# Counting edges into a table: the running counts re-added by TensorE, copied back by ScalarE, in two interleaved runs of pairs

## The chip, the core and the metric

The kernel runs on one core of a Trainium2 chip. The metric is device time of that core in microseconds (us), the median of several runs. TensorE multiplies, VectorE (DVE in the rows), ScalarE (ACT) and GpSimd (POOL) compute element by element, SyncE (SP) starts transfers. SBUF is the on-chip memory with 128 partitions; PSUM is the memory into which TensorE writes, here 8 banks.

## What is computed

A graph of 3125 nodes and 103,125 directed edges (sorted by destination, self-loops included) goes through four message-passing layers with a residual and a normalisation each. Cut to one layer's use of the graph:

```python
deg = segment_sum(ones_like(col), col, num_segments=N)
norm = deg_inv_sqrt[row] * deg_inv_sqrt[col]
msg = norm[:, None] * h[row]
agg = segment_sum(msg, col, num_segments=N)
```

Layer 0 does this three times, layer 1 and layer 2 once each with other weights, layer 3 is an attention over edges. The kernel turns the sums over edges of layers 0 to 2 into dense products with a table of counts, `edges`: how many edges lead from source node s to destination node d. Building that table is what the change touches.

## The kernel before

`program` runs stages one after the other, each in blocks that end with a barrier of all engines: `build_edges`, `degrees`, `edge_groups`, `layer0`, `layer1_nodes`, `layer1_sum`, `layer1_post`, `layer2`, `attention`. No work of a later stage starts inside the build.

`edges` lies in SBUF as [128 partitions, 25 tiles, 3136 columns] in bf16: source node s is partition s mod 128 and tile s div 128, the column is the destination. Columns are cut into 196 strips of W = 16. The edge list is cut into 403 groups of 256 edges. Since it is sorted, a group touches one strip or a few neighbours, and a (group, strip) combination that can hold edges is a *pair*: 598 of them, padded to 600, in ascending order of group and strip. Neighbouring pairs mostly share a group or a strip.

`build_edges` first prepares. VectorE computes for each pair its group (`gidx`) and its strip (`first`, `stripI`), by comparing `cuts` with the pair's number. GpSimd fetches source and destination of each pair's edges by indirect DMA once `b_pairs` is given, then blanks half of `edges` (L229); VectorE blanks the other half (L267), waits for GpSimd's half, writes the identity into the table, and computes for each edge `lo` = source mod 128 (in `loT`) and `q` = (source div 128) x 16 + column within the strip (in `qT`), a value outside the 400 columns of `qcol` for an edge that belongs to another strip. SyncE brings the strips into `strip`, from which engines read registers.

Then the loop, 15 turns (`TURNS`) of 40 pairs (`BODY`), unrolled within a turn. For each pair, and each half of 128 edges in it (edges on partitions):

- ScalarE makes `lo_hot` [128 edges, 128], one where the column equals `lo`: |lane - lo| (L311) for 20 pairs, then one pass 1 - x clipped at zero over all 20 (L315). `lo_hot` has two sets of 20 pairs.
- VectorE makes `q_hot` [128 edges, 400], one where `qcol` equals `q` (L327), in a ring of 4 pairs (`QRING`).
- TensorE multiplies the two, both halves into the same PSUM bank `acc` (L357): counts of this pair for 128 x 400 cells.
- VectorE adds the bank into the 25 x 16 cells of the strip in `edges` (L336), two pairs behind its compares, each add waiting for the one before (`added`).

The semaphore `multiplied` counts products, `q_ready` and `lo_ready` the hot tiles, `added` the adds. Each engine works off its own queue in order. The strip's column is a register that VectorE loads from `strip`, four at a time (L342). `layer1_sum` is touched only in which tiles hold two of its sums.

## Time and profile before

| | us |
|---|---|
| median of 3 runs | 3228.88 (3228.57 to 3230.82) |
| the profiled execution, its own time | 3229.49 |
| its span in the trace | 3227.6 |
| busy in the span: PE, DVE, ACT, POOL | 2528.7, 2415.7, 1858.7, 1387.2 |
| mean granted TensorE clock over the span | 0.743 |

Times in rows count from the span's start. PE is TensorE's matmuls, PEld its weight loads, which overlap them; PEclk is the granted clock as a share of 2.4 GHz, so 0.50 is 1.2 GHz and 1.00 is 2.4 GHz. The length of an instruction reaches from its start to its end, and the next one on the same engine can start before that end, so the pace of an engine is read from one start to the next. What stands in brackets behind a row is how long the engine was idle before it and what ended that. Waits, register and branch instructions don't count as busy.

### The profile page before, as it was taken

The page shows a single profiled execution, that of the slowest core. Times are in us where ns is not written, and L with a number is a line of the kernel's source. Part 1 is how long each engine was busy: PE and PEld are TensorE (multiplying, and loading weights), DVE is VectorE, ACT ScalarE, POOL GpSimd, SP SyncE. Part 2 cuts the span into 40 slices and gives each one's busy share as a digit, 9 for nine tenths or more (in the row PEclk, how much of TensorE's full clock was granted, in tenths as well). Part 3 has the DMA queues.
Part 4 walks back from the last instruction along what each step waited for, and adds up shares of the span by engine and source line. Part 5 has one row for each costly group of instructions (what it writes and reads, how often), then busy time and mean ns, then how long its engine had stood idle before and what let it go on. Part 6 is the DMA issues. An engine that isn't in the chain of part 4 may idle for free. (4 is left out here: it accounts for less than half of the span.)

```text
span 3227.6 us, 40266 instructions
## 1 busy us (share of the span) xinstructions
PE 2528.7 (78%) x7498; PEld 984.6 (31%) x7498; DVE 2415.7 (75%) x4210; ACT 1858.7 (58%) x7322; POOL 1387.2 (43%) x1220
## 2 busy tenths in 40 slices
PE   0877888886873869985598899898999899899950
PEld 0111111133452535533133333333333333333320
DVE  5999999943111445502499999999999999999967
ACT  2888888800000111110678878878878878888820
POOL 3000000005765300000777767777677767777403
PEclk9566555577975889997587788778777778778775
DMA  1000000002332454430122222222222222222113
GB/s 17 0 0 0 0 0 0 0 3 68 89 86 79 135 175 147 145 109 13 27 64 68 82 62 70 78 65 70 78 66 70 78 65 70 74 70 70 66 52 87
DMA packets 122245, 201.39 MB, mean 62 GB/s; under 512 B 55143, under 2 KB 76536, under 8 KB 116320
## 3 DMA queue, kind: packets, MB, share of 16 engines
q1 hardware_dynamic: 84192, 170.52, 15.2%
q0 software_dynamic: 38016, 30.45, 5.5%
q8 instruction: 15, 0.25, 0.0%
q14 instruction: 22, 0.18, 0.0%
HBM read 72.73 MB, written 128.17 MB: 62 GB/s over the span
## 5 line engine op out<-in xcount | busy, mean ns | idle before, releaser
L1463 POOL DMA_INDIRECT hs<-h_table,gix x880 | 1090.1, 1239 | 426.8 <-issue 251.4
L1557 ACT ACTIVATE e<-wps,hs 128x32 f32<-128x32 f32 x5632 | 1015.8, 651 | 187.0 <-PE wps L1487 145.8
L1487 PE MATMUL wps<-w_edge,ef 18*128 18x512 f32 x1760 | 682.7, 856 | 199.0 <-DVE e L1595 77.9
L1509 PE MATMUL slot_sums<-e,ident 128*128 128x512 f32 x1408 | 728.0, 671 | 7.6 <-DVE e L1660 7.6
L357 PE MATMUL acc<-q_hot,lo_hot 128*128 128x400 bf16 x1200 | 470.6, 496 | 131.2 <-DVE q_hot L327 68.1
L1509 PEld LDWEIGHTS slot_sums<-e,ident 128*128 128x128 f32 x1408 | 291.6, 216 | 467.2 <-issue 441.3
L1487 PEld LDWEIGHTS wps<-w_edge,ef 18*128 18x128 f32 x1760 | 229.3, 238 | 610.9 <-ACT e L1557 270.0
L311 ACT ACTIVATE lo_hot<-lane,loT 128x128 bf16<-128x128 f32 x1200 | 353.7, 386 | 19.8 <-PE acc L357 19.6
L1595 DVE TENSOR_TENSOR e<-wps,hs 128x1024 f32<-128x1024 f32 (+1 forms) x220 | 309.3, 1431 | 70.9 <-PE wps L1487 70.9
L336 DVE TENSOR_TENSOR edges<-acc,edges 128x400 f32 x600 | 338.5, 564 | 22.6 <-PE acc L357 16.8
L327 DVE TENSOR_SCALAR q_hot<-qcol,qT 128x400 bf16<-128x400 bf16 x1200 | 325.8, 313 | 5.3 <-issue 4.1
L497 POOL IOTA q_laneI<- 128x256 int32 x1 | 0.3, 341 | 669.9 <-ACTq L494 669.9
L439 POOL DMA_INDIRECT got<-in_edge_rows,ix x224 | 225.9, 1009 | 100.7 <-issue 54.0
L1660 DVE TENSOR_TENSOR e<-e 128x1024 f32<-128x1024 f32 x220 | 253.5, 1216 | 0.0
L1642 DVE TENSOR_TENSOR e<-e,shifts 128x1024 f32<-128x1024 f32 x220 | 253.4, 1217 | 0.0
L357 PEld LDWEIGHTS acc<-q_hot,lo_hot 128*128 128x128 bf16 x1200 | 78.9, 109 | 522.6 <-DVE q_hot L327 501.4
L1018 PE MATMUL acc<-edges,msg_parts 128*128 (+1 forms) x1050 | 210.5, 356 | 25.2 <-DMA msg_parts<-msg 25.2
L1567 ACT ACTIVATE e<-e 128x1024 f32<-128x1024 f32 x220 | 227.5, 1234 | 3.2 <-DVE e L1642 0.7
L628 PE MATMUL acc<-edges,parts 128*128 x875 | 173.5, 363 | 48.2 <-DVE mean L752 20.9
L1045 ACT COPY efT<-tr 128x512 f32<-128x512 f32 x56 | 32.8, 585 | 213.4 <-PE tr L1027 213.4
L1018 PEld LDWEIGHTS acc<-edges,msg_parts 128*128 128x128 bf16 x1050 | 103.3, 98 | 113.4 <-DMA msg_parts<-msg 25.6
L1209 POOL MEMSET blank<- 1x512 f32 x1 | 0.5, 514 | 319.0 <-POOLq L1108 319.0
(305 smaller groups left out, 2033.3 us busy)
## 6 DMA issues: line engine op xcount, KB each, us to landing
rows_state<-states SPq DMA_DIRECT2D x44, 1280.0 KB, 4.6
rows_shift<-shifts SPq DMA_DIRECT2D x44, 640.0 KB, 3.0
edges_order<-got SPq DMA_DIRECT2D x56, 256.0 KB, 2.5
got_order<-edges_order SPq DMA_DIRECT2D x56, 256.0 KB, 2.9
ef_order<-efT SPq DMA_DIRECT2D x56, 256.0 KB, 3.0
hs<-h_table,gix POOLq DMA_INDIRECT x880
ef<-ef_order SPq DMA_DIRECT2D x44, 320.0 KB, 3.0
msg<-m_parts SPq DMA_DIRECT2D x10, 480.0 KB, 4.9
```

What stands on the lines that cost most here:

```text
L311: ins = nc.scalar.activation(lo_hot[:, u, s, k, :], lane[:, :], ACT.Abs, bias=loT[:, s, bass.ds(i * BODY + u * UNROLL + k, 1)])
L327: ins = nc.vector.tensor_scalar(q_hot[:, k % QRING, s, :], qcol[:, :], qT[:, s, bass.ds(i * BODY + k, 1)], None, ALU.is_equal)
L336: nc.vector.tensor_tensor(cell, acc[:, k % BANKS, 0:QW].rearrange("p (t w) -> p t w", w=W), cell, ALU.add).then_inc(added, 1)
L357: ins = nc.tensor.matmul(acc[:, k % BANKS, 0:QW], lo_hot[:, k // UNROLL, s, k % UNROLL, :], q_hot[:, k % QRING, s, :], start=(s == 0), sto ...
L1018: ins = nc.tensor.matmul(acc[:, bass.ds(j - f * CHUNKS, 1), 0:CW], parts[:, f, k, a, :], edges[:, k, bass.ds((j - f * CHUNKS) * CW, CW)], ...
L1463: nc.gpsimd.indirect_dma_start(out=hs[u][:, s, :], out_offset=None, in_=d["h_table"], in_offset=bass.IndirectOffsetOnAxis(ap=gix[u][:, s:s ...
L1487: nc.tensor.matmul(wps[:, bank, :], ef[u][k:k + KM, g * P:(g + 1) * P], w[k:k + KM, :], start=True, stop=True).then_inc(a_mult, 1)
L1509: ins = nc.tensor.matmul(sums[:, g % 2, :], ident[:, :], e[u][:, g * SLOTS + c, :], start=(c == 0), stop=(c == SLOTS - 1))
L1557: ins = nc.scalar.mul(e[u][:, s, at], wps[:, bank, at], hs[u][:, s, f:f + 1])
L1595: nc.vector.tensor_tensor(e[u][:, s0:s1, :].rearrange("p s (i c) -> p (s i) c", c=2 * F), wps[:, bank:bank + s1 - s0, :].rearrange("p s (i ...
L1642: nc.vector.tensor_tensor(e2, e2, bc(shift(u, g), 1, SLOTS), ALU.subtract).then_inc(a_sub, 1)
L1660: ins = nc.vector.tensor_tensor(pair[:, :, 1, :], pair[:, :, 0, :], pair[:, :, 1, :], ALU.mult)
```

## The change

- The add on VectorE goes. TensorE, after the two products of a pair, multiplies the identity (`ident_b`, bf16) with the strip's present 400 cells of `edges` into the same PSUM bank, so that the bank holds old counts plus new ones. ScalarE copies the bank over those cells.
- ScalarE no longer makes `lo_hot`. VectorE does, by a compare of `lane` (now bf16) with `loT`, as it does for `q_hot`. Both are rings of 5 pairs (`HOTS`). The loop on VectorE holds four compares a pair and one wait.
- The product of pair k with the identity waits for ScalarE's copy of pair k-2 (`taken`), ScalarE's copy of k for the product (`multiplied`). TensorE and ScalarE read the strip's column into registers, five at a time.
- Pairs are taken in two runs: 0 to 299 and 300 to 599, one from each in turn, so that two pairs in a row don't touch the same strip. For the one strip that both runs share (`middle`), the second run counts into a spare strip behind the table (16 more columns, so rows of `edges` are 3152 long), and VectorE adds that strip to its place once at the end. The preparation computes the new order and that strip.
- `layer1_sum` uses `indeg` and a slice of `deg` in place of two tiles of its own.

```diff
-UNROLL = 20
-BODY = 2 * UNROLL
+RUNS = 2
+HOTS = 5
+BODY = 8 * HOTS
 TURNS = -(-PAIRS // BODY)
+RUN = TURNS * BODY // RUNS
...
-            keep["edges"] = graph.enter_context(nc.sbuf_tensor("edges", [P, TILES, COLS], BF16))
+            keep["edges"] = graph.enter_context(nc.sbuf_tensor("edges", [P, TILES, COLS + W], BF16))
...
-        lane = sb("lane", [P, P])
+        lane = sb("lane", [P, P], BF16)
         qcol = sb("qcol", [P, QW], BF16)
-        strip = sb("strip", [1, PAIR_TILES * P], I32)
+        strip = sb("strip", [1, (PAIR_TILES + 1) * P], I32)
+        ident_b = sb("ident_b", [P, P], BF16)
...
-                    v.add(nc.vector.tensor_copy(pair[:, :], pairI[:, :]))
+                    v.then(nc.vector.tensor_scalar(turnI[:, :], pairI[:, :], 1, None, ALU.bitwise_and))
+                    v.then(nc.vector.tensor_scalar(pairI[:, :], pairI[:, :], 1, None, ALU.arith_shift_right))
+                    v.then(nc.vector.tensor_copy(own[:, :], turnI[:, :]))
+                    v.then(nc.vector.tensor_copy(pair[:, :], pairI[:, :]))
+                    v.then(nc.vector.scalar_tensor_tensor(pair[:, :], own[:, :], float(RUN), pair[:, :],
+                                                          ALU.mult, ALU.add))
...
+                    v.then(nc.vector.tensor_scalar(below[:, :], cuts[:, :], float(RUN), None, ALU.is_le))
+                    v.then(nc.vector.tensor_reduce(middle[:, :], below[:, :], X, ALU.add))
+                    v.then(nc.vector.tensor_scalar(middle[:, :], middle[:, :], -1.0, float(RUN), ALU.mult, ALU.add))
...
-                    v.then(nc.vector.tensor_scalar(stripI[:, :], first[:, :], float(STRIPS - 1), float(W),
-                                                   ALU.min, ALU.mult))
+                    v.then(nc.vector.tensor_scalar(apart[:, :], first[:, :], middle[:, 0:1], None, ALU.is_equal))
+                    v.then(nc.vector.tensor_tensor(apart[:, :], apart[:, :], own[:, :], ALU.mult))
+                    v.then(nc.vector.tensor_scalar(own[:, :], first[:, :], float(STRIPS - 1), None, ALU.min))
+                    v.add(nc.vector.tensor_scalar(stripI[:, PAIR_TILES:PAIR_TILES + 1], middle[:, :], float(W), None,
+                                                  ALU.mult))
+                    v.then(nc.vector.scalar_tensor_tensor(apart[:, :], own[:, :], float(-STRIPS), apart[:, :],
+                                                          ALU.add, ALU.mult))
+                    v.then(nc.vector.tensor_tensor(own[:, :], own[:, :], apart[:, :], ALU.subtract))
+                    v.then(nc.vector.tensor_scalar(stripI[:, 0:PAIR_TILES], own[:, :], float(W), None, ALU.mult))
...
+                    dve.wait_ge(b_consts, 2)
+                    v.add(nc.vector.tensor_copy(ident_b[:, :], ident[:, :]))
...
-                    nc.vector.tensor_scalar(t2[:, :, :], dstg[:, :, :], -1.0, None, ALU.mult).then_inc(b_cast, 1)
+                    nc.vector.tensor_copy(t2[:, :, :], dstg[:, :, :]).then_inc(b_cast, 1)
...
-        lo_hot = sb("lo_hot", [P, 2, 2, UNROLL, P], BF16)
-        q_hot = sb("q_hot", [P, QRING, 2, QW], BF16)
+        lo_hot = sb("lo_hot", [P, HOTS, 2, P], BF16)
+        q_hot = sb("q_hot", [P, HOTS, 2, QW], BF16)
         acc = ctx.enter_context(nc.psum_tensor("acc", [P, BANKS, 512], F32))
-        lo_far, lo_ready, q_ready = sem("lo_far"), sem("lo_ready"), sem("q_ready")
-        multiplied, added = sem("multiplied"), sem("added")
+        hot, multiplied, taken, joined = sem("hot"), sem("multiplied"), sem("taken"), sem("strips_joined")
         with nc.Block() as block:
-            @block.scalar
-            def _(act):
-                with act.Fori(0, TURNS) as i:
-                    for u in range(2):
-
-                        act.wait_ge(multiplied, i * BODY + (u + 1) * UNROLL)
-
-                        for k in range(UNROLL):
-                            for s in range(2):
-                                ins = nc.scalar.activation(lo_hot[:, u, s, k, :], lane[:, :], ACT.Abs,
-                                                           bias=loT[:, s, bass.ds(i * BODY + u * UNROLL + k, 1)])
-                        ins.then_inc(lo_far, 1)
-                        act.wait_ge(lo_far, i * 2 + (u + 1))
-                        nc.scalar.activation(lo_hot[:, u, :, :, :], lo_hot[:, u, :, :, :], ACT.Relu,
-                                             scale=-1.0, bias=1.0).then_inc(lo_ready, 1)
-
             @block.vector
             def _(dve):
-                dve.sem_inc(added, BANKS)
-                strips = [dve.alloc_register(f"strip{k}") for k in range(BODY)]
                 with dve.Fori(0, TURNS) as i:
-                    def one_hot(k):
-
-                        dve.wait_ge(multiplied, i * BODY + (BODY + k + 1 - QRING))
+                    for k in range(BODY):
+
+                        dve.wait_ge(multiplied, i * BODY + (BODY + k + 1 - HOTS))
                         for s in range(2):
-                            ins = nc.vector.tensor_scalar(q_hot[:, k % QRING, s, :], qcol[:, :],
-                                                          qT[:, s, bass.ds(i * BODY + k, 1)], None, ALU.is_equal)
-                        ins.then_inc(q_ready, 1)
-
-                    def add(k):
-                        s16 = dve.snap(strips[k], min_val=0, max_val=COLS - W)
-                        dve.wait_ge(multiplied, i * BODY + (BODY + k + 1))
-                        dve.wait_ge(added, i * BODY + (BANKS + k))
-                        cell = edges[:, :, bass.ds(s16, W)]
-                        nc.vector.tensor_tensor(cell, acc[:, k % BANKS, 0:QW].rearrange("p (t w) -> p t w", w=W),
-                                                cell, ALU.add).then_inc(added, 1)
-
-                    for k in range(BODY):
-                        one_hot(k)
-                        if k % 4 == 0:
-                            dve.load(strips[k:k + 4], strip[0:1, bass.ds(i * BODY + k, 4)])
-                        if k >= 2:
-                            add(k - 2)
-                    add(BODY - 2)
-                    add(BODY - 1)
+                            at = bass.ds(i * BODY + k, 1)
+                            nc.vector.tensor_scalar(lo_hot[:, k % HOTS, s, :], lane[:, :], loT[:, s, at], None,
+                                                    ALU.is_equal)
+                            ins = nc.vector.tensor_scalar(q_hot[:, k % HOTS, s, :], qcol[:, :], qT[:, s, at], None,
+                                                          ALU.is_equal)
+                        ins.then_inc(hot, 1)
+
+                dve.wait_ge(taken, RUNS + TURNS * BODY)
+                shared = dve.value_load(strip[0:1, PAIR_TILES * P:PAIR_TILES * P + 1], min_val=0, max_val=COLS - W)
+                cell = edges[:, :, bass.ds(shared, W)]
+                nc.vector.tensor_tensor(cell, cell, edges[:, :, COLS:COLS + W], ALU.add).then_inc(joined, 1)
 
             @block.tensor
             def _(pe):
                 pe.sem_inc(multiplied, BODY)
+                cells = [pe.alloc_register(f"cell{k}") for k in range(HOTS)]
                 with pe.Fori(0, TURNS) as i:
                     for k in range(BODY):
-                        pe.wait_ge(lo_ready, i * 2 + (k // UNROLL + 1))
-                        pe.wait_ge(q_ready, i * BODY + (k + 1))
-                        pe.wait_ge(added, i * BODY + (k + 1))
+                        if k % HOTS == 0:
+                            pe.load(cells, strip[0:1, bass.ds(i * BODY + k, HOTS)])
+                        s16 = pe.snap(cells[k % HOTS], min_val=0, max_val=COLS)
+                        total = acc[:, k % BANKS, 0:QW]
+                        pe.wait_ge(hot, i * BODY + (k + 1))
                         for s in range(2):
-                            ins = nc.tensor.matmul(acc[:, k % BANKS, 0:QW],
-                                                   lo_hot[:, k // UNROLL, s, k % UNROLL, :],
-                                                   q_hot[:, k % QRING, s, :], start=(s == 0), stop=(s == 1))
-                        ins.then_inc(multiplied, 1)
+                            nc.tensor.matmul(total, lo_hot[:, k % HOTS, s, :], q_hot[:, k % HOTS, s, :],
+                                             start=(s == 0), stop=False)
+
+                        pe.wait_ge(taken, i * BODY + (k + 1))
+                        nc.tensor.matmul(total, ident_b[:, :], edges[:, :, bass.ds(s16, W)],
+                                         start=False, stop=True).then_inc(multiplied, 1)
+
+            @block.scalar
+            def _(act):
+                act.sem_inc(taken, RUNS)
+                cells = [act.alloc_register(f"cell{k}") for k in range(HOTS)]
+                with act.Fori(0, TURNS) as i:
+                    for k in range(BODY):
+                        if k % HOTS == 0:
+                            act.load(cells, strip[0:1, bass.ds(i * BODY + k, HOTS)])
+                        s16 = act.snap(cells[k % HOTS], min_val=0, max_val=COLS)
+                        act.wait_ge(multiplied, i * BODY + (BODY + k + 1))
+                        nc.scalar.copy(edges[:, :, bass.ds(s16, W)],
+                                       acc[:, k % BANKS, 0:QW].rearrange("p (t w) -> p t w", w=W)
+                                       ).then_inc(taken, 1)
...
-        rowsum, raw = sb("rowsum", [P, TILES]), sb("outdeg", [P, TILES])
+        rowsum, raw = keep["indeg"], deg[:, 1, :]
```

TensorE's queue in the loop, one pair before (the two matmuls of a pair are the halves of its edges):

```order
L354 REGISTER_ALU [waits lo_ready]
L357 MATMUL acc<-q_hot,lo_hot 128x400 [waits added,q_ready]
L357 MATMUL acc<-q_hot,lo_hot 128x400
L354 REGISTER_ALU [waits lo_ready]
L357 MATMUL acc<-q_hot,lo_hot 128x400 [waits added,q_ready]
L357 MATMUL acc<-q_hot,lo_hot 128x400
```

and pairs of the changed kernel, from the first of five, whose strips `strip` holds:

```order
L350 TENSOR_LOAD strip
L351 ISA
L355 MATMUL acc<-q_hot,lo_hot 128x400 [waits hot]
L355 MATMUL acc<-q_hot,lo_hot 128x400
L359 ISA [waits taken]
L359 MATMUL acc<-edges,ident_b 128x400
L351 ISA
L355 MATMUL acc<-q_hot,lo_hot 128x400 [waits hot]
L355 MATMUL acc<-q_hot,lo_hot 128x400
L359 ISA [waits taken]
L359 MATMUL acc<-edges,ident_b 128x400
```

Ahead of the third matmul, the one with `ident_b`, now stands an instruction that waits for `taken`, and the next pair's matmuls stand behind it; once in five pairs there is a TENSOR_LOAD.

VectorE's queue in the loop, before (two compares, then the add of two pairs earlier):

```order
L325 REGISTER_ALU
L327 ISA [waits multiplied]
L327 TENSOR_SCALAR q_hot<-qcol,qT 128x400
L327 ISA
L327 TENSOR_SCALAR q_hot<-qcol,qT 128x400
L332 ISA
L334 REGISTER_ALU [waits multiplied]
L336 ISA [waits added]
L336 TENSOR_TENSOR edges<-acc,edges 128x25x16
```

and one pair of the changed kernel:

```order
L332 ISA [waits multiplied]
L332 TENSOR_SCALAR lo_hot<-lane,loT 128x128
L334 REGISTER_ALU
L334 TENSOR_SCALAR q_hot<-qcol,qT 128x400
L332 ISA
L332 TENSOR_SCALAR lo_hot<-lane,loT 128x128
L334 REGISTER_ALU
L334 TENSOR_SCALAR q_hot<-qcol,qT 128x400
L329 REGISTER_ALU
```

The add and its two waits are gone; a compare for `lo_hot` stands ahead of each for `q_hot`.

ScalarE's queue at the start of a turn in the changed kernel, where `multiplied` is the signal of a finished bank:

```order
L369 TENSOR_LOAD strip
L370 ISA
L372 ISA [waits multiplied]
L372 ACT_TABLE_LOAD
L372 COPY edges<-acc 128x25x16
L370 ISA
L372 ISA [waits multiplied]
L372 COPY edges<-acc 128x25x16
```

Forty activations and a pass over 20 pairs are replaced by a copy a pair; the table load stands in the turn as it did before, now between the wait for the turn's first product and its copy.

## Rows read from the trace of the kernel before

**Rows 1.** The page, busy tenths in 40 equal slices of the span.

```profile
DVE  5999999943111445502499999999999999999967
...
PEclk9566555577975889997587788778777778778775
```

**Rows 2.** Busy us by window: length, then busy (count) per engine, PEclk, DMA share, GB/s.

```profile
62.00:664.00 602.00, 470.61 (x1200) 78.92 (x1200) 574.34 (x1800) 506.93 (x1245) 0.00 (x0) 0.58 0.00 0
665.60:669.00 3.40, 3.40 (x11) 1.36 (x10) 0.00 (x0) 0.00 (x0) 0.00 (x0) 0.50 0.55 53
669.00:700.00 31.00, 31.00 (x165) 15.95 (x163) 3.67 (x6) 0.00 (x0) 0.00 (x0) 1.00 0.00 0
303.80:307.20 3.40, 3.10 (x8) 0.46 (x8) 3.40 (x12) 3.37 (x9) 0.00 (x0) 0.50 0.00 0
307.20:310.70 3.50, 2.06 (x9) 0.45 (x8) 3.50 (x12) 3.37 (x1) 0.00 (x0) 0.99 0.00 0
310.70:314.10 3.40, 1.30 (x5) 0.26 (x4) 2.75 (x8) 1.80 (x7) 0.00 (x0) 0.50 0.00 0
```

**Rows 3.** Groups by line, 62 to 664 us: busy us, mean ns, idle before, releasers.

```profile
L357 PE MATMUL acc<-q_hot,lo_hot 128*128 128x400 bf16 x1200 | 470.6, 496 | 131.2 <-DVE q_hot L327 68.1 <-ACT lo_hot L315 19.1
L311 ACT ACTIVATE lo_hot<-lane,loT 128x128 bf16<-128x128 f32 x1200 | 353.7, 386 | 19.8 <-PE acc L357 19.6
L336 DVE TENSOR_TENSOR edges<-acc,edges 128x400 f32 x600 | 338.5, 564 | 22.6 <-PE acc L357 16.8 <-DVE edges L336 5.8
L327 DVE TENSOR_SCALAR q_hot<-qcol,qT 128x400 bf16<-128x400 bf16 x1200 | 325.8, 313 | 5.3 <-issue 4.1 <-PEq L350 0.7
```

**Rows 4.** Timeline of 302.18 to 304.2 us: start, length, engine, idle before.

```profile
302.19 0.54 DVE L327 TENSOR_SCALAR q_hot<-qcol,qT 128x400 bf16<-128x400 bf16 x2
302.65 0.56 DVE L336 TENSOR_TENSOR edges<-acc,edges 128x400 f32 x1
302.79 0.13 PEld L357 LDWEIGHTS acc<-q_hot,lo_hot 128*128 128x128 bf16 x2 [0.81 <-DVE q_hot L327]
303.14 0.54 DVE L327 TENSOR_SCALAR q_hot<-qcol,qT 128x400 bf16<-128x400 bf16 x2
```

**Rows 5.** Timeline of VectorE, first and last pairs of the build.

```profile
62.51 0.56 DVE L327 TENSOR_SCALAR q_hot<-qcol,qT 128x400 bf16<-128x400 bf16 x2 [0.70 <-PEq L350]
...
82.16 0.56 DVE L336 TENSOR_TENSOR edges<-acc,edges 128x400 f32 x1
...
663.40 0.57 DVE L336 TENSOR_TENSOR edges<-acc,edges 128x400 f32 x1 [0.20 <-DVE edges L336]
```

**Rows 6.** Timeline of VectorE, 718.45 to 719.3 us (a later stage).

```profile
718.46 0.25 DVE L560 TENSOR_SCALAR hi_hot<-q_lane,q_hi 128x128 bf16<-128x128 bf16 x1
718.63 0.27 DVE L561 TENSOR_SCALAR glo_hot<-q_lane,q_lo 128x220 bf16<-128x220 bf16 x1
```

**Rows 7.** ScalarE copies out of PSUM: group by line, then a timeline near 1302 us.

```profile
L1053 ACT COPY agg_stage<-acc 128x448 f32 (+1 forms) x14 | 7.4, 532 | 4.4 <-PE acc L1018 4.4
...
1301.71 0.60 PE L1027 MATMUL tr<-ident,got_order 128*128 128x128 f32 x4
...
1302.35 0.58 ACT L1045 COPY efT<-tr 128x512 f32<-128x512 f32 x1 [3.37 <-PE tr L1027]
```

**Rows 8.** Timeline of ScalarE at the start of a turn.

```profile
332.29 1.28 ACT L311 ACT_TABLE_LOAD   x1 [3.69 <-PE acc L357]
333.58 0.40 ACT L311 ACTIVATE lo_hot<-lane,loT 128x128 bf16<-128x128 f32 x1
```

**Rows 9.** Timeline of VectorE in the preparation.

```profile
11.14 0.64 DVE L259 TENSOR_SCALAR below<-cuts,pair 128x403 f32<-128x403 f32 x1
...
12.42 0.17 DVE L261 TENSOR_SCALAR gidx<-gidx 128x5 f32<-128x5 f32 x1
12.62 0.17 DVE L262 CAST gidxI<-gidx 128x5 int32<-128x5 f32 x1
...
41.85 3.44 DVE L274 CAST edges<-ident 128x128 bf16<-128x128 f32 x25 [7.34 <-POOL edges L229]
```

19 lines of the change are left out of this document (11 added, 8 removed).

## The prediction

> **What bounds the kernel now.** The page of the profile comes first: the slices of PEclk and VectorE [rows 1]. The span is 3227.6 us, and slices two to eight (81 to 645 us) have VectorE at 9 and TensorE's clock at 5 or 6 tenths. The stretches by window [rows 2] say the same: from 62 to 664 us VectorE is busy 574.3 of 602 us, ScalarE 506.9, TensorE 470.6 by durations, at a mean granted clock of 0.58. The groups by line [rows 3] give three kinds of work for the 600 pairs (15 turns of 40): 1200 `q_hot` compares and 600 adds of `acc` into `edges` on VectorE, 1200 `lo_hot` activations on ScalarE and 1200 matmuls on TensorE. The timeline [rows 4] shows who waits. VectorE goes from the first of two compares (302.19) to the add (302.65) in 0.46 us, from the add to the next compare (303.14) in 0.49, with no idle time; TensorE's weight load has waited 0.81 us for `q_hot`. So VectorE is the bound, at 0.95 us a pair, and what TensorE and ScalarE do in between is covered. Nothing after the build overlaps it (blocks are separated by a barrier), so what the build gives goes straight into the span.
>
> How much of the build is that pace: the second add starts at 82.16, the 600th at 663.40 [rows 5], 581.2 us for 598 steps. 598 x 0.948 is 566.9; the other 14.3 us lie at 14 boundaries between turns, about 1.0 us each. Before the first adds stand 19.6 us (62.51 to 82.16 [rows 5]), in which VectorE waits for ScalarE's first block of 40 activations and the Relu pass behind them.
>
> **What the change does to VectorE.** It loses the add: 0.49 us a pair that read PSUM and wrote `edges`. It gains two compares of 128 columns for `lo_hot`, now bf16 from a bf16 `lane`. The trace has this very form in a later stage: a compare of 128 x 128 bf16 with a scalar per partition starts at 718.46, the next instruction at 718.63 [rows 6], 0.16 to 0.17 us; I take 0.165. Starts are what counts here, since durations (0.25) overlap the next one. A pair is then 2 x 0.23 + 2 x 0.165 = 0.79 us, and 600 pairs 474 us. Both ends of the unknown: that row has no address registers between instructions, as the loop will have. The 400-column compare that has them takes 0.23; were that the floor for the small one too, a pair would be 0.92. From below, 0.15 would give 0.76.
>
> **TensorE.** Two matmuls of 400 columns become three. From 669 to 700 us 165 matmuls of 448 columns ran in 31.0 us at clock 1.00, 0.188 each; scaled to 400 columns that is 0.168 at 2.4 GHz, and twice that, 0.335, at 1.2 GHz [rows 2]. Three cost 0.50 or 1.0 us a pair. At 2.4 GHz TensorE is well under VectorE's 0.79, at 1.2 GHz above it, so the clock decides. The trace tells this much. The build's two matmuls a pair fill 0.67 of 0.95 us at 1.2 GHz (303.8 to 307.2); after that the clock was 0.99 (307.2 to 310.7), where the same work fills only 0.34 of 0.95, and then it fell again (310.7 to 314.1, with a boundary's pause in it) [rows 2]. A saturated TensorE at 1.2 GHz was raised (665.6 to 669 at 0.50, then 669 to 700 at 1.00) and while saturated stayed up. In the changed loop TensorE at 1.2 GHz is saturated (1.0 wanted, 0.79 offered), so I expect it to be raised; at 2.4 GHz it fills 0.50 of 0.79, in between, so it may fall again. Alternating halves are harmless: equal times at 1.0 and at a catching-up pace of 0.65 (below) do 1.00 + 1.54 pairs in 2 us, 0.79 a pair, and the ring of five hot pairs lets VectorE run on through a low stretch. Such a loop would go on at VectorE's pace, with little to spare.
>
> A rule speaks against this part: the Trainium skill, "TensorE: Matmul & The Clock Gate", Part 3, section "The mechanism", says a weight load overlaps matmuls in flight only where the row group differs. Here all three loads use all rows, so each matmul would be preceded by its load. The trace disagrees: 163 loads with 15.95 us of their own lie inside the 31.0 us in which TensorE was busy throughout [rows 2], and 0.188 is what the columns alone explain. By the trace a pair is 0.50 us; by the rule, with 0.10 us for each load, 0.80.
>
> **The new chain.** The identity product of pair k reads the cell that ScalarE wrote for pair k-2 (the two runs alternate), and pair k+2 needs what ScalarE copies from k. One round of two pairs: a matmul start to end, 0.34 to 0.54 us (0.50 is the mean of the build's mix [rows 3]); ScalarE starts 0.04 after TensorE's end (1302.31 to 1302.35 [rows 7]), plus a register instruction ahead on its queue, which no row prices alone: nothing from below, from above the 0.20 that VectorE's 600th add waits for the end of the add before it [rows 5]; I take 0.1; the copy, between the 0.53 us of 448 columns and, by the slope to 512 (0.58), 0.49 for 400 [rows 7]; back to TensorE 0.06 (302.73 to 302.79 [rows 4]) plus another 0.1. That is 1.1 to 1.3 us per two pairs, 0.57 to 0.65 a pair. ScalarE itself is busy 0.49. Neither shows beside 0.79. Register loads of five strips on TensorE and ScalarE stand every fifth pair; the trace's page has no price for them. From below they are hidden (TensorE waits 0.3 us a pair anyway). From above they cost what a boundary on VectorE costs, 1.0 us per five pairs, which would take a saturated TensorE to 0.7 or 1.2 a pair. I take them as hidden, with the 0.65 above as catching-up pace.
>
> **Boundaries, start and end.** At each turn ScalarE loads its activation table inside the loop, 1.28 us, with the first activation 1.29 after its start [rows 8]. Now it stands between the wait for the first product and its copy, so the chain loses about 1.3 us plus a branch, 15 times. VectorE has up to five pairs of lead less the 2 us that a pair takes from compare to product; what is left covers most, and I charge 0.7 us for each of 14 boundaries, 10 us (none and 1.5, so 0 and 21, are the ends). The "ScalarE: Activation LUTs" page of the Trainium skill, section "What ACT_TABLE_LOAD costs", adds a drain of some 1.38 us at a switch to another set. This trace shows no such time behind the load, and the sum doesn't use it; with it the boundaries would cost up to 21 us more.
>
> At the start VectorE is no longer kept waiting: the 19.6 us go. At the end the last pair drains: two matmuls and the identity product at 1.2 GHz (0.67 + 0.54), the copy (0.49), signals 0.3, then the join, a register read and an add of 0.56 [rows 4], together 3.3 us.
>
> From 62.51, where the first compare starts: 474 + 10 + 3.3 = 487. Before: to the end of the 600th add, 663.97, 601.5. **Gain 114.2.**
>
> **Preparation.** Waited VectorE instructions on five columns are 0.20 apart (12.42 to 12.62), the pair of `below` and its reduction 1.28 (11.14 to 12.42) [rows 9]. New ahead of `b_pairs`: four more at the top (0.8), one compare with reduction and a small one (1.5), and seven for one behind (1.1). 3.4 us, all on the path, because GpSimd's gathers and its memset of half of `edges` start behind `b_pairs` and VectorE waits 7.34 us for that memset at 41.85 [rows 9]. The `ident_b` cast costs 0.14 (3.44 over 25), 16 more columns on 3136 0.1. Loss 3.6 us. VectorE's own memset shifts under GpSimd's and costs nothing: it ended before the 7.34 us of waiting. Later stages read `edges` with a longer row and get two reused tiles: nothing, in either direction.
>
> **Sum.** The profiled execution took 3229.5 us. 3229.5 - 114.2 + 3.6 = 3118.9; the median of the runs is 0.6 lower: **3118 us**.
>
> **Rivals.**
> 1. Small compare at the floor of the large one, 0.23: a pair 0.92, 600 x 0.13 = 78 us more, 3196. For it: address registers between all compares. Against: neighbours on five and on 128 columns do come closer. Chance 0.09.
> 2. TensorE and ScalarE set the pace, at 0.87 (register loads exposed, clock changing): 48 us more, 3166. For it: the thin margin above, and TensorE's queue in which the next pair's matmuls stand behind an identity product that waits. Against: lead of five pairs. Chance 0.14.
> 3. Slower: the clock stays at 1.2 GHz. Then 1.0 us a pair, and nothing to catch up with at boundaries: 600 + 15 x 2 + 3.3 = 633 against 601.5, plus 3.6, 3265. It decides once the mean pair costs more than (601.5 - 3.6 - 3.3) / 600 = 0.99 us, boundaries included. Against: saturation raised the clock at 669. Chance 0.05.
> 4. Weight loads in series, the skill's rule: 0.80 at 2.4 GHz, 1.3 at 1.2; between those 1.0, 3245. Chance 0.01.
> 5. Forecast: VectorE's pace of 0.77 to 0.82 with boundaries of 0 to 1.5 us, 3100 to 3148. Chance 0.71.
>
> Case 5 with most of case 2, and nothing of case 1, makes the range 3098 to 3172, which leaves out a little under 2 in 10. A change of 0.2% (6.5 us) is about what a measurement of this kernel can tell. Faster by more than that: 0.94 (cases 5, 2, 1). Slower: 0.05. Within: 0.01.
>
> **What would show it.** In the build, four VectorE compares every 0.79 us with no `edges` row of VectorE but one; `lo_hot` to `q_hot` 0.165 apart. TensorE's clock between 0.6 and 0.9 there, idle before it put down to `q_hot` or `lo_hot`. ScalarE's copies near 0.49, 600 of them. First compare near 66, `ones_b` of the next stage near 554. Wrong, if VectorE shows idle time behind `acc` in the middle of a turn (case 2 or 3), or if compares are more than 0.2 apart (case 1).

## The result, and the profile after

The changed kernel takes **3143.6 us** in the median (3141.0 to 3149.0, four runs) against 3229.6 us before (3228.6 to 3230.8, four runs): ratio 0.974, 95% interval 0.972 to 0.975. That is 86 us faster. The forecast was 3118 us, 111 us faster, with 3098 to 3172 as its range. The direction and the range hold, and so does VectorE's pace; 25 us of the forecast gain are missing, and this section and the next find where they went.

The groups by line of the changed kernel, 60 to 600 us, answer to [rows 3] (busy us, mean ns of one | idle us before, with releasers):

```profile
L334 DVE TENSOR_SCALAR q_hot<-qcol,qT 128x400 bf16<-128x400 bf16 x1200 | 380.3, 317 | 0.4 <-issue 0.4
L355 PE MATMUL acc<-q_hot,lo_hot 128*128 128x400 bf16 x1200 | 317.9, 348 | 133.0 <-DVE q_hot L334 129.1 <-issue 1.0
L332 DVE TENSOR_SCALAR lo_hot<-lane,loT 128x128 bf16<-128x128 bf16 x1200 | 296.9, 247 | 31.1 <-PE acc L359 30.5 <-PEq L345 0.6
L372 ACT CAST edges<-acc 128x400 f32 x600 | 291.9, 493 | 170.5 <-PE acc L359 153.0
L359 PE MATMUL acc<-edges,ident_b 128*128 x600 | 209.9, 350 | 9.1 <-ACT edges L372 8.9
...
L372 ACT ACT_TABLE_LOAD x15 | 19.2, 1283 | 94.3 <-PE acc L359 94.3
```

The adds on VectorE are gone, 1200 small compares have come, and the 600 copies on ScalarE take 0.49 us each. But VectorE, which the forecast had busy throughout, has a wait of its own: 31 us ahead of `lo_hot`.

The windows, to be read beside [rows 2]:

```profile
100.00:200.00 100.00, 70.95 (x360) 31.15 (x360) 95.30 (x480) 61.71 (x123) 0.00 (x0) 0.98 0.00 1
...
300.00:400.00 100.00, 73.67 (x355) 32.15 (x353) 92.70 (x467) 60.63 (x120) 0.00 (x0) 0.93 0.00 1
...
307.20:310.60 3.40, 3.13 (x12) 1.31 (x12) 3.40 (x19) 1.64 (x4) 0.00 (x0) 0.67 0.00 0
310.60:330.00 19.40, 13.85 (x74) 6.32 (x73) 19.40 (x100) 12.14 (x25) 0.00 (x0) 1.00 0.00 1
```

TensorE's clock stayed at its upper level for most of the build (a mean of 0.93 to 0.98 in stretches of 100 us), where before the mean was 0.58. VectorE is 5 to 7 us in a hundred short of busy. The timeline across one turn of VectorE's loop shows where those are (start, length, engine, idle before; 299 to 307.5 us):

```profile
300.05 0.33 PE L359 MATMUL acc<-edges,ident_b 128*128 x1
300.05 0.27 PEld L355 LDWEIGHTS acc<-q_hot,lo_hot 128*128 128x128 bf16 x2
...
300.21 0.50 PE L355 MATMUL acc<-q_hot,lo_hot 128*128 128x400 bf16 x2
...
300.39 0.10 PEld L359 LDWEIGHTS acc<-edges,ident_b 128*128 128x128 bf16 x1
...
300.55 0.33 PE L359 MATMUL acc<-edges,ident_b 128*128 x1
...
300.77 0.32 DVE L334 TENSOR_SCALAR q_hot<-qcol,qT 128x400 bf16<-128x400 bf16 x1
...
302.19 0.34 PE L359 MATMUL acc<-edges,ident_b 128*128 x1
303.45 0.25 DVE L332 TENSOR_SCALAR lo_hot<-lane,loT 128x128 bf16<-128x128 bf16 x1 [2.36 <-PE acc L359]
303.62 0.32 DVE L334 TENSOR_SCALAR q_hot<-qcol,qT 128x400 bf16<-128x400 bf16 x1
303.85 0.25 DVE L332 TENSOR_SCALAR lo_hot<-lane,loT 128x128 bf16<-128x128 bf16 x1
304.01 0.32 DVE L334 TENSOR_SCALAR q_hot<-qcol,qT 128x400 bf16<-128x400 bf16 x1
304.25 0.25 DVE L332 TENSOR_SCALAR lo_hot<-lane,loT 128x128 bf16<-128x128 bf16 x1
...
305.18 1.28 ACT L372 ACT_TABLE_LOAD   x1 [2.04 <-PE acc L359]
```

Two things are to be seen. Inside a turn the pace is 0.79 to 0.80 us a pair (303.45 to 304.25), with 0.16 to 0.17 from `lo_hot` to `q_hot`: the forecast's two numbers. And at 303.45, the head of the turn, VectorE has stood for 2.36 us. The profile puts that down to `acc`. But the first compare of a turn needs only the product of five pairs earlier, and that is the identity product which starts at 300.05 and takes 0.33 us; at 302.19 even the last product of the turn is under way. Whatever held VectorE until 303.45, it was not the signal it is put down to.

The build is best read as one length, from the first compare (65.98) to `ones_b` of the next stage (577.9), 511.9 us. Of it 600 pairs at 0.792 us are 475.2, and the end (from 574.0, when VectorE is through with its last pair: last product, copy, join, barrier) is 3.9. The remaining **33 us lie at 14 boundaries**, 2.3 us each, for which the forecast had 10 us, 0.7 each. That is the missing gain. `ones_b` stood at 664.3 before, so the build and its preparation gave 86.4 us. In the profiled execution the stages behind the build took 6 us more than before (2569.3 against 2563.3 of spans of 3147.2 and 3227.6), but it was the slowest of its four runs; the medians, 86.0 apart, show no such loss.

### The profile page after: what moved, and what is told of

Same layout as the page of the kernel before. It is cut to its first block and busy times, and to the rows that moved or that the text cites. A ratio compares the mean times of both kernels' runs of the same rounds, so it can differ in the third digit from the quotient of the medians.

```text
span 3147.2 us, 41487 instructions
## 1 busy us (share of the span) xinstructions
PE 2434.3 (77%) x8098; PEld 1066.8 (34%) x8099; DVE 2324.1 (74%) x4824; ACT 1666.9 (53%) x6693; POOL 1385.3 (44%) x1220
## 5 line engine op out<-in xcount | busy, mean ns | idle before, releaser
L355 PE MATMUL acc<-q_hot,lo_hot 128*128 128x400 bf16 x1200 | 317.9, 348 | 133.0 <-DVE q_hot L334 129.1
L372 ACT CAST edges<-acc 128x400 f32 x600 | 291.9, 493 | 170.5 <-PE acc L359 153.0
L334 DVE TENSOR_SCALAR q_hot<-qcol,qT 128x400 bf16<-128x400 bf16 x1200 | 380.3, 317 | 0.4 <-issue 0.4
L332 DVE TENSOR_SCALAR lo_hot<-lane,loT 128x128 bf16<-128x128 bf16 x1200 | 296.9, 247 | 31.1 <-PE acc L359 30.5
L359 PE MATMUL acc<-edges,ident_b 128*128 x600 | 209.9, 350 | 9.1 <-ACT edges L372 8.9
L355 PEld LDWEIGHTS acc<-q_hot,lo_hot 128*128 128x128 bf16 x1200 | 101.5, 100 | 226.1 <-DVE q_hot L334 180.2
```

Source lines behind the costliest of these rows:

```text
L332: nc.vector.tensor_scalar(lo_hot[:, k % HOTS, s, :], lane[:, :], loT[:, s, at], None, ALU.is_equal)
L334: ins = nc.vector.tensor_scalar(q_hot[:, k % HOTS, s, :], qcol[:, :], qT[:, s, at], None, ALU.is_equal)
L355: nc.tensor.matmul(total, lo_hot[:, k % HOTS, s, :], q_hot[:, k % HOTS, s, :], start=(s == 0), stop=False)
L372: nc.scalar.copy(edges[:, :, bass.ds(s16, W)], acc[:, k % BANKS, 0:QW].rearrange("p (t w) -> p t w", w=W)).then_inc(taken, 1)
```

## The experiments

Two theories for the boundary. **Jump**: VectorE's branch back to the head of its loop is slow, because its instructions have to be fetched again. **Stop in the chain**: ScalarE's table load stands between the turn's first product and its copy, TensorE then waits for ScalarE, and the five hot pairs of lead don't cover it. The page's DMA queues speak for the jump. In the kernel before, queue 14, which fetches instructions, moved 22 packets, 0.18 MB; in the changed kernel (packets, MB, share):

```profile
q14 instruction: 92, 0.75, 0.1%
```

That is 70 fetches of 8 KB more, five a turn for 14 turns. Two of the five come directly behind the branch, the other three in the course of the next turn; the two of the turn shown above, between 299.5 and 303.5 us:

```profile
q14 instruction: 2, 0.02, 2.2%
```

Counted in the traces, one turn of VectorE's queue is 346 instructions before and 362 now.

The experiments ran on other chips, on which the stages behind the build take 150 to 210 us longer whatever the kernel (the kernel before: 3436, 3380 and 3376 us in the three groups). The changed kernel itself ran again on the second of the three, and there its build is the same, 512.5 us against 511.9; on the other two only the pace within a turn can be compared, 0.792 us a pair in every kernel here with four compares, except in experiment 4. So each ratio is to the kernel before on the same chip, and builds are compared by their own length. "Lost at boundaries" is that length less 475.2 and 3.9.

### 1. VectorE's loop alone in turns of 20 pairs

```
-                with dve.Fori(0, TURNS) as i:
-                    for k in range(BODY):
+                with dve.Fori(0, 2 * TURNS) as i:
+                    for k in range(BODY // 2):
```

The same work from half the code, with the indices in the loop to match; it has 30 turns, TensorE and ScalarE still have 15.

> The changed kernel with VectorE's loop alone cut to 30 turns of 20 pairs; TensorE and ScalarE keep 15 turns of 40. Theory A (VectorE's jump back at a turn's end, 3.6 us in the trace of the changed kernel, is an instruction fetch, because the unrolled body of 40 pairs doesn't stay in its instruction buffer): with half the body the jump costs the 0.3 us it cost before the change, which the work queued ahead hides; the 14 boundaries of 2.35 us go, 33 us, less up to 5 for what ScalarE's table load then still does; total 3143.6 - 28 to 33, so 3111 to 3116 us, and no instruction fetches per turn in the DMA rows. Theory B (the boundary is ScalarE's table load and TensorE's branch and register load, for which VectorE waits): turns of TensorE and ScalarE are as they were, so 3143 us as in the changed kernel.

Measured: 3329.9 us (3326.2 to 3344.6), ratio 0.968 (0.965 to 0.972). Build 497.2 us, 15 less; lost at boundaries 18 instead of 33. With twice the branches, the 70 fetches are gone:

```profile
q14 instruction: 21, 0.17, 0.0%
```

So the jump is real, but it isn't all. The timeline of this kernel at a turn of TensorE and ScalarE shows the rest:

```profile
298.00 1.28 ACT L372 ACT_TABLE_LOAD   x1 [1.12 <-PE acc L359]
...
299.29 0.89 ACT L372 CAST edges<-acc 128x400 f32 x2
...
299.92 0.34 PE L359 MATMUL acc<-edges,ident_b 128*128 x1 [1.19 <-ACT edges L372]
...
302.52 0.51 PE L355 MATMUL acc<-q_hot,lo_hot 128*128 128x400 bf16 x2 [1.17 <-DVE q_hot L334]
...
303.35 0.26 DVE L332 TENSOR_SCALAR lo_hot<-lane,loT 128x128 bf16<-128x128 bf16 x1 [0.47 <-PE acc L359]
...
305.01 0.34 PE L359 MATMUL acc<-edges,ident_b 128*128 x1
306.55 0.51 PE L355 MATMUL acc<-q_hot,lo_hot 128*128 128x400 bf16 x2 [1.20 <-DVE q_hot L334]
...
310.55 0.51 PE L355 MATMUL acc<-q_hot,lo_hot 128*128 128x400 bf16 x2 [1.17 <-DVE q_hot L334]
```

The table load (298.00) holds the copy; the identity product waits 1.19 us for it; then, at 302.52, TensorE stands again, and now VectorE waits 0.47 at the end of its ring. The second pause is put down to `q_hot`, which had been given long before. It recurs every five pairs, at the head of each group that loads five strips into registers. TensorE's register loads in the changed kernel, by source line (ns: shortest, median, longest; first and last start):

```profile
L350 PEldq TENSOR_LOAD <-strip x120: 583/1233/1247, 66.1 to 571.3; - x120
```

1.23 us, where the forecast had them hidden or, from above, 1.0. And they leave TensorE next to no time to catch up. From the first product of one group of five pairs to that of the next it takes 4.03 and 4.00 us (302.52, 306.55, 310.55), VectorE's five pairs 3.96. TensorE waits for nothing of VectorE's there: in this kernel its first product starts within about 0.2 us of the end of the register load in all 120 groups. Only where the five strips begin on a multiple of 16 bytes, twice a turn, is the load 0.59 us, and the group that ends with it 3.4 to 3.8. So here it is TensorE's side, and not VectorE, that sets the length of a turn, 32.6 us against VectorE's 31.7.

A part of the 18 us is the clock. In four of the 14 turns it fell behind the pause at the boundary, and those took 33.9 us in place of 32.6, 5.5 us in all. The window of one, 268.5 to 271.9 us, has it at 0.51:

```profile
268.50:271.90 3.40, 3.33 (x11) 1.52 (x12) 2.27 (x12) 1.02 (x3) 0.00 (x0) 0.51 0.00 0
```

### 2 and 3. TensorE and ScalarE in turns of 20; then all three

```
-BANKS = 8
+BANKS = 5
...
-                with pe.Fori(0, TURNS) as i:
-                    for k in range(BODY):
+                with pe.Fori(0, 2 * TURNS) as i:
+                    for k in range(HALF):
```

and the same for ScalarE, which so loads its table 30 times. The ring of banks falls to five, so that 20 pairs are whole rounds of it. Experiment 3 has the edit of experiment 1 as well.

> The mirror image: TensorE's and ScalarE's loops cut to 30 turns of 20 pairs (PSUM banks used 5 in place of 8, so that 20 is a multiple), VectorE's kept at 15 turns of 40. Theory A: VectorE's 14 boundaries of 2.35 us stay, and the 15 further branches and table loads of the others hide under VectorE's pace: 3143 us, up to 3150. Theory B: twice as many boundaries of 2.35 us: 3143 + 33, so 3176 us.

> Both of the other two edits: all three engines in 30 turns of 20 pairs, 5 PSUM banks. Theory A: as VectorE's cut alone, 3111 to 3118 us, 30 table loads hidden by VectorE's lead. Theory B: 30 boundaries: 3176 us.

Measured: 3367.9 us, ratio 0.979 (0.975 to 0.983), build 532.8 us, lost 54; and 3358.2 us, ratio 0.976 (0.972 to 0.979), build 519.8 us, lost 41. Against the changed kernel's 512 that is 21 us and 8 us more: less than the 33 of theory B, and not what theory A had either (0 to 7 more, and 25 to 32 less). Against experiment 1, which has the same VectorE loop, experiment 3 loses 23 us more for 15 more turns, 1.5 us each. So a turn of the TensorE and ScalarE loops has a price of its own, whatever VectorE does. The edit changes three things at once (table loads, branches, banks) and can't say which of them it is (experiment 7 moves the table load alone). More fetches it is not. The page of experiment 3 has 100 more of them on queue 14 than that of experiment 1:

```profile
q14 instruction: 121, 0.99, 0.1%
```

but only 2 of the 121 lie in its build (66 to 585 us) and 118 behind it, where experiment 1 has 18. The stages behind the build are the same code in both; what differs is how much code stands ahead of them.

### 4. One run of pairs

```
-                    v.then(nc.vector.tensor_scalar(turnI[:, :], pairI[:, :], 1, None, ALU.bitwise_and))
-                    v.then(nc.vector.tensor_scalar(pairI[:, :], pairI[:, :], 1, None, ALU.arith_shift_right))
+                    v.then(nc.vector.tensor_scalar(turnI[:, :], pairI[:, :], 0, None, ALU.bitwise_and))
+                    v.then(nc.vector.tensor_scalar(pairI[:, :], pairI[:, :], 0, None, ALU.arith_shift_right))
...
-                act.sem_inc(taken, RUNS)
+                act.sem_inc(taken, 1)
```

Pairs are taken in order, so each identity product needs the copy of the pair just before.

> The changed kernel with pairs in one run in ascending order, so that the identity product of pair k waits for ScalarE's copy of pair k-1 and not k-2. It measures the chain of product, copy and product. The prediction has one round at 1.1 to 1.3 us: 600 x (1.2 - 0.79) is 246, so 3330 to 3450 us, slower than before the change (3229), with VectorE waiting for TensorE throughout. Rival: the round is shorter than VectorE's 0.79 us because TensorE runs the two hot products in its shadow and signals cost little; then the order is worth nothing and the time stays at 3143 us.

Measured: 3638.1 us (3622.6 to 3658.5), ratio 1.056 (1.051 to 1.062), build 808.9 us. The timeline of this kernel in the middle of a turn:

```profile
303.05 0.34 PE L359 MATMUL acc<-edges,ident_b 128*128 x1 [0.40 <-ACT edges L372]
...
303.50 0.49 ACT L372 CAST edges<-acc 128x400 f32 x1 [0.58 <-PE acc L359]
...
304.12 0.34 PE L359 MATMUL acc<-edges,ident_b 128*128 x1 [0.40 <-ACT edges L372]
```

One round is 1.07 to 1.08 us: 0.34 for the product, 0.11 to the copy, 0.49, and 0.13 back to TensorE. The prediction had 1.1 to 1.3. The interleave is what the change lives by: without it the kernel is 5.6% slower than before. 600 rounds are 648 us; the rest of the 809 weren't taken apart. In them are boundaries and register loads, which stand in the open here, and stretches at the lower clock (its mean from 66 to 870 us is 0.78).

### 5. Four products a pair

To experiment 1 a repeated first product is added; it gives the same sums, since the second start overwrites the first.

```
-                        for s in range(2):
+                        for n, s in enumerate((0, 0, 1)):
...
-                                             start=(s == 0), stop=False)
+                                             start=(n < 2), stop=(n == 0))
```

> The kernel with VectorE's turns of 20, and on TensorE the first hot product of each pair made twice (the bank is started anew by the second), four matmuls a pair in place of three, 0.167 us more at 2.4 GHz. The first experiments left 18 us of waits in the build and showed TensorE working off five pairs in a burst of 2.6 us, then standing for a register load of 1.23 us. Theory C (TensorE's side, five pairs plus one load, takes 3.9 to 4.0 us and is as long as VectorE's 5 x 0.79 = 3.96, so there is no slack at all): 0.167 more a pair, 600 x 0.167 = 100 us more, build 497 + 100 = 597 us. Rival (VectorE's pace binds and TensorE has 0.2 us or more to spare, as the prediction had it): no more than 10 us, build under 507.

Measured: 3322.5 us (3319.0 to 3324.3), ratio 0.983 (0.981 to 0.984), build 539.9 us. VectorE now waits in the middle of turns too, once in five pairs (timelines of VectorE and of TensorE in this kernel):

```profile
306.03 0.26 DVE L332 TENSOR_SCALAR lo_hot<-lane,loT 128x128 bf16<-128x128 bf16 x1 [0.27 <-PE acc L359]
...
310.48 0.26 DVE L332 TENSOR_SCALAR lo_hot<-lane,loT 128x128 bf16<-128x128 bf16 x1 [0.40 <-PE acc L359]
...
314.92 0.25 DVE L332 TENSOR_SCALAR lo_hot<-lane,loT 128x128 bf16<-128x128 bf16 x1 [0.39 <-PE acc L359]
```

```profile
305.03 0.68 PE L355 MATMUL acc<-q_hot,lo_hot 128*128 128x400 bf16 x3 [0.92 <-DVE q_hot L334]
...
308.25 0.33 PE L359 MATMUL acc<-edges,ident_b 128*128 x1
309.48 0.68 PE L355 MATMUL acc<-q_hot,lo_hot 128*128 128x400 bf16 x3 [0.89 <-DVE q_hot L334]
```

So TensorE's side takes 4.45 us for five pairs, at a clock of 1.00 in the mean from 66 to 540 us. A product is 0.167 us there, so the fourth adds 0.835 in five pairs; yet the 4.45 are only 0.45 more than the 4.00 of experiment 1, and 43 us come out in place of 100. The other half goes into time that was idle. With three products the five pairs stand 0.50 to 0.57 us apart, since some identity products wait for the copy of two pairs before, and the first product of a group is 2.49 us ahead of the last identity product (302.52 to 305.01 above); with four it is 3.22 (305.03 to 308.25), 0.73 more. And from there to the next group it is 1.23 us in place of 1.54, because the register load runs beside products that are still queued.

Neither expectation held. The rival's 0.2 us to spare a pair isn't there: a group of five took 4.00 us against VectorE's 3.96 already in experiment 1, as theory C said. What theory C had wrong is that the time on TensorE's side is not a sum of products and load alone. The forecast's catching-up pace of 0.65 us a pair was 0.80 in most groups.

### 6. Strips loaded four at a time

Three kernels on one chip share their runs of the kernel before: the changed kernel unedited, this edit alone, and this edit with that of experiment 1. The loads then are of four numbers, 16 bytes, on a multiple of 16.

```
-                cells = [pe.alloc_register(f"cell{k}") for k in range(HOTS)]
+                cells = [pe.alloc_register(f"cell{k}") for k in range(4)]
...
-                        if k % HOTS == 0:
-                            pe.load(cells, strip[0:1, bass.ds(i * BODY + k, HOTS)])
+                        if k % 4 == 0:
+                            pe.load(cells, strip[0:1, bass.ds(i * BODY + k, 4)])
```

and the same on ScalarE.

> The changed kernel itself, unedited, beside the others of this group on one chip, because the runs before it came from a chip on which the stages behind the build take some 210 us longer. From VectorE's first compare to the next stage's first instruction: 512 us, as in its first trace (66.0 to 577.9).

> The changed kernel with the strips of TensorE and ScalarE loaded four at a time every fourth pair, so that each load starts on a multiple of 16 bytes, in place of five every fifth. In the trace of the changed kernel loads at pairs 0, 20 took 0.585 us, those at pairs 5, 10 and 15 took 1.23. Theory C: a load of four falls to 0.34, as VectorE's loads of four had before the change, TensorE's side to (4 x 0.52 + 0.45) / 4 = 0.63 us a pair, and what its own and ScalarE's boundary cost, about 1.0 of 2.35 us a turn, is caught up: build 512 - 15 = 497 us; VectorE's jump remains. Rival (load length is that of a busy engine, not of alignment): loads stay at 1.2 and come more often, TensorE's side at (4 x 0.52 + 1.3) / 4 = 0.85, build 540 us.

> Both mended: register loads of four and VectorE's turns of 20 pairs. Theory A with C: nothing is left but VectorE's pace, 600 x 0.792 = 475, plus drain and barrier of 4: build 480 us against 512 of the changed kernel, so 32 us less than it in all. If each of the two causes had only hidden behind the other, less than the sum: over 490.

Measured: unedited 3295.3 us (ratio 0.975, 0.974 to 0.977), build 512.5 us. Four at a time 3282.5 us (0.971, 0.969 to 0.973), build 503.1, lost 24 (497 was expected). With VectorE's 20 pairs as well **3262.0 us (0.964, 0.962 to 0.966), build 478.4, lost nothing**. The register load by source line, of the kernel with loads of four alone:

```profile
L350 PEldq TENSOR_LOAD <-strip x150: 328/333/529, 66.0 to 563.0; - x150
```

about a quarter of the time for four strips that it took for five. And the groups of VectorE in the kernel with both edits:

```profile
L334 DVE TENSOR_SCALAR q_hot<-qcol,qT 128x400 bf16<-128x400 bf16 x1200 | 397.8, 331 | 0.0
L332 DVE TENSOR_SCALAR lo_hot<-lane,loT 128x128 bf16<-128x128 bf16 x1200 | 314.8, 262 | 0.6 <-PEq L345 0.6
```

No wait for `acc` is left. The table load is still there, 15 times, and costs nothing now. So with short register loads TensorE makes the stop of 1.3 us good within the turn, its first full groups of four pairs behind a boundary taking 2.5 to 2.9 us where VectorE's take 3.17 (kernel with both edits); with a load of 1.23 us in most groups it can't. The edit shortens ScalarE's loads as well (1.12 us in the median in the changed kernel), but in the timeline of experiment 1 those are hidden: the copy at 303.31 starts 0.11 us after its product's end at 303.20, as in the middle of a turn. The two edits give 9 and 15 us alone and 34 together: while VectorE stands for its jump, TensorE's stop passes unseen, so mending one uncovers part of the other.

### 7. Table load ahead of the wait

Does the table load itself make the remaining 18 us of experiment 1? Strips stay at five a load; VectorE has turns of 20; a copy of one element into a tile that nobody reads stands at the head of ScalarE's turn, so that the table comes in before any wait.

```
                 with act.Fori(0, TURNS) as i:
+                    nc.scalar.copy(scratch[:, :], ones[0:1, 0:1])
                     for k in range(BODY):
```

> The kernel with VectorE's turns of 20, register loads of five as in the change, and on ScalarE a copy of one element at the head of each turn, ahead of the register load and the wait for the first product, so that the table load of 1.28 us is done while TensorE branches, loads registers and multiplies. The kernel without that copy lost 18 us in the build to boundaries of the other two engines. If the table load is what makes those (theory), 1.28 x 14 = 18 us go, build 497 - 15 to 18 = 479 to 482 us. If they are TensorE's branch and register load (rival), the build stays at 497 us.

Measured: 3254.8 us (3245.1 to 3262.4), ratio 0.964 (0.961 to 0.967), build 478.3 us, nothing lost. The timeline at a turn of this kernel:

```profile
289.45 1.28 ACT L368 ACT_TABLE_LOAD   x1
...
289.99 0.33 PE L360 MATMUL acc<-edges,ident_b 128*128 x1
...
290.75 0.19 ACT L368 COPY scratch<-ones 1x1 f32<-1x1 f32 x1
...
290.84 0.86 ACT L374 CAST edges<-acc 128x400 f32 x2
```

The load begins 0.02 us after ScalarE's previous copy (288.94 and 0.49), without a wait, while TensorE is at its register load and the turn's first products. The first copy starts at 290.84, 0.5 us after its product's end (290.32); in experiment 1 it started at 299.29, 1.4 us after its product's end (297.89). The table load in the chain was the stop: with register loads of 1.23 us still there, taking most of it out of the way is enough. How much room that leaves isn't shown; groups of five still take 4.00 us on TensorE's side.

### 8. A fifth compare

With nothing lost any more, is VectorE's pace the bound? To experiment 6's last kernel one more 128-column compare a pair is added, into a tile that nobody reads.

> The kernel with both mends (loads of four, VectorE's turns of 20) and one compare of 128 columns more a pair on VectorE, into a tile that nobody reads: five compares in place of four. VectorE's pace is the bound (theory): the pace goes from 0.792 to 0.792 + 0.165 = 0.957 us, the build from 478 to 478 + 99 = 577 us. Rival (VectorE's pace is set by something else, its register instructions or TensorE's signal, and a compare of 128 columns costs less than its 0.165): less than 60 us more.

Measured: 3351.7 us (3342.3 to 3356.9), ratio 0.992 (0.990 to 0.995), build 575.8 us, 97 us more than without it, 0.162 us a pair. The timeline of VectorE in this kernel:

```profile
302.89 0.24 DVE L333 TENSOR_SCALAR lo_hot<-lane,loT 128x128 bf16<-128x128 bf16 x1
303.06 0.24 DVE L336 TENSOR_SCALAR spare<-lane,loT 128x128 bf16<-128x128 bf16 x1
303.22 0.31 DVE L338 TENSOR_SCALAR q_hot<-qcol,qT 128x400 bf16<-128x400 bf16 x1
...
303.85 0.24 DVE L333 TENSOR_SCALAR lo_hot<-lane,loT 128x128 bf16<-128x128 bf16 x1
```

The compare added shows in full: in this kernel VectorE bounds the loop and everything else is covered. It also confirms the 0.165 of [rows 6], now with address registers between.

## Why the prediction was right, and where it was off

- **VectorE's pace**: 0.79 forecast, 0.792 measured; a small compare 0.165 forecast, 0.162 by experiment 8. Rival 1 (0.23, 3196 us) is out. That most of the saving came through to the result also took some luck, told below with rival 2.
- **TensorE**: three matmuls fit at the upper clock, as argued. In the timeline of a turn shown first, three products with their three weight loads follow each other every 0.50 us (300.05 to 300.55), three times the 0.17 that came out of [rows 2]. Rival 4, with three weight loads in series, would have them 0.3 us longer; three loads lie inside that 0.50 (300.05, two in a row, and 300.39). The rule behind it, from the Trainium skill, "TensorE: Matmul & The Clock Gate", Part 3, section "The mechanism", the trace contradicts a second time; but the same section also lets a load go ahead of matmuls in flight when it goes to the background weight buffer, which the prediction left out. The clock was 0.93 to 0.98, above my 0.6 to 0.9: it fell back behind the pauses at boundaries (0.67 from 307.2 to 310.6 us, 1.00 to 330), and was 1.00 in the kernels of experiments 6 (both edits) and 7, which lose nothing there. Rival 3 needed the lower level throughout.
- **The chain**: 1.1 to 1.3 us a round forecast, 1.08 measured, copy 0.49 as said.
- **Preparation, start and drain**: loss 3.6 us forecast, 3.5 measured (first compare 62.51 before, 65.98 after); end 3.3 forecast, 3.9 with the barrier. Together they are within 1 us.
- **Boundaries**: the term that was mis-sized, 10 us forecast with 21 at most, 33 measured. Two steps failed in it. First, VectorE's own branch got no price of its own, only ScalarE's table load did; nothing in the forecast asked whether the longer loop body would be fetched again. Second, "Register loads of five strips... I take them as hidden, with the 0.65 above as catching-up pace": they take 1.23 us and are not hidden. With them TensorE's side needs 4.00 us where VectorE needs 3.96, so little is left with which to make good a table load (the two short groups of a turn gain some 0.7 us against 3.96), and that, with the clock's falls behind it, is 18 us without the jump. A price was to be had from below: VectorE's loads of four strips in the trace of before (L342) took 0.34 us in the median. Both steps are shown by removal: experiment 6 and experiment 7 each bring the 33 us back, by different ways.
- Rival 2 (TensorE and ScalarE set the pace, at 0.87, 3166 us) was nearer than its chance of 0.14 says. Its cause, exposed register loads, is real: TensorE's side ran at 0.80 a pair in groups with a long load, next to VectorE's 0.79, and in experiment 1 it set the length of every turn. That the two came out so close is luck; nothing in the prediction had it.

What the runs don't settle is why the branch takes so long. The fetches of queue 14 come and go with it inside the build, in the kernels with 362 instructions a turn (74 of them in the changed kernel's build and as many in that of experiment 2) and not in those with 346 or with 182 (3, and 2 in experiment 1). That the fetch is what holds the branch was not tested apart from it. The Trainium skill, "Runtime: NRT & Kernel Launch", section "Instruction fetch mechanics", says that a taken branch whose target isn't in the window held at that time has to fetch it first. The trace agrees in kind; the page gives room for 512 instructions on such an engine and fetches of 16 KB, while here a body of 362 already pays, and the fetches are of 8 KB (0.75 MB over 92). Length may not be all: where the body stands in the engine's code changed as well, and in experiments 2 and 3 some 100 fetches more appear in later stages whose own code is unchanged (117 and 118 against 18). A longer body and the same body in another place are rivals that no run here separates.

The best kernels of the study are those of experiments 6 (both edits) and 7, 34 us under the changed kernel in the build (478.4 and 478.3 us against 512.5), with ratios of 0.964 to the kernel before, where the changed kernel has 0.975 on one of the same chips. Both edits of experiment 6 together with the table load taken out early were not run; nothing is left at the boundaries for it to give.

## What to carry to other kernels

When one engine of a loop is sped up, look at what each of the others needs for the same stretch of work, register loads and waits for each other included: here TensorE's side needed 4.00 us where VectorE needed 3.96, and with so little between them a stop of 1.3 us once a turn can't be made good. After a change of a loop's body look at the instruction queue's packets, and at their times, beside the waits. A wait that the profile puts down to a product or a tile which had been ready for microseconds is something that the profile doesn't name; here it was a branch once and a register load once. Find what stands in a chain once a turn (table loads, register loads), shorten it or move it to where the engine idles anyway; and try such mends together, since here each hid part of the other.

## What the hardware showed that I had not expected

- The branch back on VectorE held its next compare until 2.68 us after the last `q_hot` had started (300.77 to 303.45, usually 0.23), with five fetches of 8 KB in each of 14 turns, two of them directly behind the branch; with half the code (182 instructions a turn for 362), 2 fetches in the whole build and no such stop.
- A load of registers from SBUF on TensorE takes 0.33 us for four strips on a multiple of 16 bytes and 1.23 us in the median for five; the loads of five that begin on a multiple of 16 bytes (pairs 0 and 20 of a turn) take 0.58 to 0.59 us. Four strips off such a multiple weren't tried.
- In groups of five pairs a fourth product of 0.167 us each cost TensorE's side 0.45 us and not 0.835: half of it fell into waits for ScalarE's copies and beside the register load.
- TensorE's clock was 1.00 in the mean from 66 to 540 us in the kernels of experiments 6 (both edits) and 7, with three products of 0.167 us in each 0.79 us; the forecast had expected it to fall again and again. In experiment 1, with a pause of TensorE at each boundary, it fell behind four of them.
- The table load in the loop took its 1.28 us and no more: the first operation behind it starts 1.29 to 1.30 us after it (305.18 and, in experiment 7, 289.45 to 290.75).
